# Attention and mixture-of-experts block: another order of value products, side products and the copy of av_bank within a step of the attention loop

## What is computed

```python
xn = layernorm(x)                                   # x: 8 x 512 tokens x 128, f32
h = xn @ W1 + b1                                    # 16 heads, q, k, v of 8 columns each
w = softmax(causal(q @ k.T / sqrt(8)))
att = (w @ v) @ Wp + bp
shared = (silu(xn @ sg.T) * (xn @ su.T)) @ sd.T     # 352 hidden columns
routed = sum over the 2 best of 8 experts of weight * ffn_expert(xn)
out = x + att + shared + routed
```

## Time and profile before

| | us |
|---|---|
| median of 3 runs | 559.99 |
| the runs | 559.99, 562.06, 555.53 |
| profiled execution, its own time | 559.99 |
| its span, first to last instruction | 558.3 |
| TensorE busy | 513.5 |
| mean granted TensorE clock | 0.955 |

### The profile page before, as it was taken

How to read it: one execution, slowest core, us unless ns; L and a number is a source line. 1 busy time by engine, 2 the same in 40 slices (tenths; PEclk the granted TensorE clock), 3 DMA queues, 4 the chain that set the end, 5 groups by cost and what they waited for, 6 DMA issues and landing times.

```text
span 558.3 us, 13933 instructions
## 1 busy us (share of the span) xinstructions
PE 513.5 (92%) x4584; PEld 332.5 (60%) x4585; DVE 398.1 (71%) x753; ACT 310.4 (56%) x684; POOL 324.7 (58%) x382
## 2 busy tenths in 40 slices
PE   8888999889998998899989889999999999999995
PEld 3334444444444444343443348999999999977673
DVE  7886668887878777877887675565555555548896
ACT  2016777777767767777776753333333333365542
POOL 5439742342466777767777744667666444575442
PEclk9875999999979989999997989999999999999998
DMA  5416631040211245522211112211221222434554
GB/s 166 157 46 197 211 143 65 21 154 3 77 60 44 94 170 196 176 71 90 78 54 36 49 34 65 68 57 57 73 59 57 62 70 57 119 108 130 155 153 147
DMA packets 52156, 53.46 MB, mean 96 GB/s; under 512 B 5744, under 2 KB 39568, under 8 KB 51856
## 3 DMA queue, kind: packets, MB, share of 16 engines
q1 hardware_dynamic: 47616, 43.71, 24.7%
q0 software_dynamic: 4352, 8.95, 4.8%
q10 hardware_dynamic: 144, 0.20, 0.1%
HBM read 20.38 MB, written 17.90 MB: 69 GB/s over the span
## 4 chain that ended last, share of the span: by engine, by line
PE 66%; DVE 12%; ACT 7%; issue 6%; DMA 4%; POOL 3%; DVEq 1%; SPq 0%; ACTq 0%; POOLq 0%
PE av_bank L879 13%; PE mx_pair L824 9%; PE av_bank L1053 9%; PE st_banks L852 5%; DVE neg_max L1543 4%; PE st_banks L1064 4%; DVE o_sb L1719 3%; ACT probs L1244 3%; PE av_bank L902 2%; PE st_banks L759 2%; PE mx_pair L1039 2%; DMA out<-o_sb 2%; PE mx_pair L1043 2%; PE mx_pair L1044 2%; PE mx_pair L1042 2%
## 5 line engine op out<-in xcount | busy, mean ns | idle before, releaser
L1543 DVE TENSOR_REDUCE neg_max<-mx_pair 128x2 f32<-128x256 f32 (+3 forms) x256 | 203.7, 822 | 63.4 <-PE mx_pair L835 61.0
L1244 ACT ACTIVATE probs<-st_banks 128x512 f32<-128x512 f32 (+1 forms) x384 | 181.0, 524 | 63.7 <-PE st_banks L852 62.0
L705 POOL DMA_INDIRECT y_tok<-y_sb,y_rows x72 | 70.0, 972 | 74.1 <-ACT y_sb L1349 59.6
L852 PE MATMUL st_banks<-q_st,k_st 32*128 32x128 f32 (+3 forms) x512 | 96.3, 407 | 13.4 <-ACT probs L1244 7.7
L824 PEld LDWEIGHTS mx_pair<-k_st,q_st 31*128 31x128 f32 x512 | 43.4, 190 | 101.8 <-issue 62.7
L879 PE MATMUL av_bank<-probs,v_wide 128*18 128x384 f32 (+3 forms) x1024 | 98.9, 461 | 3.5 <-ACT av_sb L1257 2.6
L824 PE MATMUL mx_pair<-k_st,q_st 31*128 31x256 f32 (+3 forms) x512 | 90.1, 395 | 11.3 <-DVE neg_max L1543 11.1
L629 POOL DMA_INDIRECT sorted_x<-xn_rows,slot_idx x64 | 63.8, 997 | 13.3 <-issue 12.7
L1342 ACT ACTIVATE sg<-mx_pair 128x352 f32<-128x352 f32 x72 | 33.4, 463 | 62.3 <-PE mx_pair L1044 62.3
L852 PEld LDWEIGHTS st_banks<-q_st,k_st 32*128 32x128 f32 x512 | 48.2, 191 | 27.5 <-ACT probs L1244 18.6
L588 POOL TENSOR_SCALAR_AFFINE_SELECT probs<-probs 128x1024 f32<-128x1024 f32 x32 | 35.0, 1094 | 45.8 <-ACT probs L1244 45.7
(11 more groups left out here) (214 smaller groups left out, 895.9 us busy)
## 6 DMA issues: line engine op xcount, KB each, us to landing
sorted_x<-zeros SPq DMA_DIRECT2D x8, 580.5 KB, 4.1
xg<-sorted_x SPq DMA_DIRECT2D x36, 129.0 KB, 2.2
picked<-y_tok SPq DMA_DIRECT2D x16, 256.0 KB, 3.7
q_st<-q_hi SPq DMA_DIRECT2D x14, 256.0 KB, 2.5
k_st<-k_hi SPq DMA_DIRECT2D x14, 256.0 KB, 2.5
egu_lo<-in_e_gu SPq DMA_DIRECT2D x2, 1408.0 KB, 6.6
x_all<-in_x SPq DMA_DIRECT2D x8, 256.0 KB, 3.6
att_T<-a_T SPq DMA_DIRECT2D x8, 256.0 KB, 2.1
```

Source lines behind the costliest of these rows:

```text
L705: pool.indirect_dma_start(y_tok, bass.IndirectOffsetOnAxis(ap=y_rows[:, t, k:k + 1], axis=0), y_sb[t % 2][:, k, :], None).then_inc(y_st[t ...
L852: ins = pe.matmul(st_banks[:, i % 3, lo:lo + w], k_st[buf][32 * j:32 * j + 32, g, kb * P:(kb + 1) * P], q_st[buf][32 * j:32 * j + 32, g, k ...
L1244: act.activation(dst, src, ACT.Exp, scale=SCALE).then_inc(st_free, 1)
L1543: ins = dve.tensor_reduce(neg_max[:, g, h:h + 2, qb], mx_pair[i % 2][:, :, lo:lo + (qb + 1) * P], AX.X, ALU.max, negate=True)
```

## The change

Three things move, in TensorE's program, in ScalarE's program and in the table that numbers the fills of st_banks:
- values(.,1) takes the place of values(.,3), and values(.,3) and (.,2) follow together behind mm2, ahead of M3.
- The first extras come ahead of M4 and the second extras ahead of M5; M5 with S(8,9) is the last of the step.
- On ScalarE the copy of av_bank goes behind exponents (6,7), and the copies of the extras follow the new order.

```diff
-        order += scored[0:4] + ([("m", s + 1)] if -1 <= s < GROUPS - 1 else []) + scored[4:10] + first_misc(s) + scored[10:12] + second_misc(s)
+        order += scored[0:4] + ([("m", s + 1)] if -1 <= s < GROUPS - 1 else []) + scored[4:8] + first_misc(s) + scored[8:10] + second_misc(s) + scored[10:12]
...
-                if kb in (1, 3):
+                if kb == 1:
                     pe.wait_ge(masked, 3 * n + 2)
...
                 if valued:
-                    values(s - 1, 3)
+                    values(s - 1, 1)
                 if maxima:
                     max_scores(s + 2, 2)
...
                 if valued:
-                    values(s - 1, 1)
+                    values(s - 1, 3)
+                    values(s - 1, 2)
                 if maxima:
                     max_scores(s + 2, 3)
                 if scored:
                     scores(s, (4, 5))
                 if maxima:
                     max_masks(s + 2, 3)
-                if valued:
-                    values(s - 1, 2)
-                if maxima:
-                    max_scores(s + 2, 4)
-                if scored:
-                    scores(s, (10, 11))
-                if maxima:
-                    max_masks(s + 2, 4)
...
                 if maxima:
-                    max_scores(s + 2, 5)
+                    max_scores(s + 2, 4)
                 if scored:
-                    scores(s, (8, 9))
+                    scores(s, (10, 11))
                 if maxima:
-                    max_masks(s + 2, 5)
+                    max_masks(s + 2, 4)
...
                 if s == 12:
                     value_bias()
+                if maxima:
+                    max_scores(s + 2, 5)
+                if scored:
+                    scores(s, (8, 9))
+                if maxima:
+                    max_masks(s + 2, 5)
...
                 if scored:
                     exponents(s, (6, 7))
+                if s >= 1 and s % GP == 0:
+                    results_out_of(s - 1)
                 if scored:
                     exponents(s, (4, 5))
-                if scored:
-                    exponents(s, (10, 11))
...
                 if s % 4 == 1 and s <= 25:
                     values_out((s + 3) // 4)
+                if scored:
+                    exponents(s, (10, 11))
...
-                if scored:
-                    exponents(s, (8, 9))
-                if s >= 1 and s % GP == 0:
-                    results_out_of(s - 1)
...
                 if s == 12:
                     bias_out()
+                if scored:
+                    exponents(s, (8, 9))
```

## The result

The change made the kernel slower: 563.44 us against 559.94 (medians of 15 runs each), ratio 1.0065 with a 95% interval of 1.0038 to 1.0093. Forecast were 558.3 us and "within 1%". The time lies just inside the range (552.8 to 563.5); the direction was wrong. The profiled execution took 564.77 us, 4.78 more than that of before, with a span of 563.0 and a mean granted clock of 0.931 against 0.955.

A forecast was written before the change was run, and what follows sets the result against it. The loop was taken as a chain of hand-overs that make TensorE wait, no engine full. Steps 1 to 25 give -1.8, later plain pairs +0.2, the start 0: in all -1.7, 559.99 to 558.3 us; range 552.8 to 563.5.

The forecast's parts named there:

- the walk: Four attention steps timed from trace durations: 34.21 us against 34.50, -1.7 in all, plain-step idle time unchanged; chance 0.47.
- Rival B: New stops in plain even steps let the clock fall in steps 8, 20, 24, 26, 30: +12, 570 us; chance 0.07.
- The price of a dip: Clock dips in the attention loop: the first costs 2.4 us, the other two about 1.2 and 2.4.
- Part 1: Moving the av_bank copy behind exponents (6,7) removes 0.33 us before values(.,0) in 15 odd steps, 5 us at most.
- Part 2: values(.,2) ahead of scores (4,5) uncovers a wait of scores (10,11): 0.5 us in plain odd steps, 0.7 in plain even.
- Parts 3 and 4: First extras (about 1.1 us) cover the wait before scores (10,11), returning part of 0.58; second extras delay M5 and exponent 8.
- The start: Steps -2 to 4, with up to two x transposes each, not walked: 0, bounded by -1 and +1 us.
- "Nothing gained" (A): Copy ahead of exponents (4,5) and uncovered scores (10,11) take back all: 560 us, 562 at worst; chance 0.25.
- the dips gone (C): The loop's three clock dips vanish as stops go and projections fill the middle: -6.0, 552.3 us; chance 0.15.
- the third mask (D): The earlier values(.,2) waits for its mask from GpSimd, 18 steps x 0.3 = +5.4: 563.7 us; chance 0.06.

The follow-up runs named there:

- after_fill5: The changed kernel plus four needless products a step in steps without first extras, ahead of scores (10,11), (8,9) and the next M0: 548.6 us, 0.9769 of before.
- hybrid: The changed kernel, but in steps without first extras values(.,2) stands last and the av_bank copy behind exponents (4,5): 577.02 us, 1.0125 of before.
- after_again: The changed kernel as it is, run again beside before on chip Q: 573.91 us, 1.008 of before.
- after_third: The changed kernel as it is, run once more beside before on chip P: 575.24 us, 1.0111 of before.
- misc_only: The kernel before with only the extras moved, values products and av_bank copy as before: 579.62 us, 1.0197 of before.
- before_stop: The kernel before, but scores (10,11) wait for one exponent more in steps from 5 on without first extras: 576.38 us, 1.0129 of before.

## Why the prediction was wrong

**The step that failed** is the sentence "My walk leaves the total idle time of a plain step as it was, so there is no term for the clock in the sum". The total was about right; that only the total mattered was not. Between the marks of step 4 and step 30, after_fill5 gives the new order at nearly full clock: 219.94 us, less some 1.5 for its one dip (steps 11 and 12), 218.4. For before, the steps with dips put at their full-clock length give 223.4. So the dips cost 231.3 - 218.4 = 12.9 us in after and 228.9 - 223.4 = 5.5 in before, +7.4, against a gain of 223.4 - 218.4 = 5.0: together the +2.4. This split is an estimate: it takes the steps of after_fill5, from another chip and with products, for those that after would have had without dips, and rests on the rows above, where the products delay nothing. Per microsecond at the lower level that is 12.9 / 34.1 = 0.38 and 5.5 / 17.1 = 0.32, so the 10.2 us more behind the loop's step 29 make 3.3 to 3.9 and explain its +3.35.

The second step that failed is the size of the gain: the walk had 1.6 for steps 4 to 29, and it was 5.0. The two errors stand against each other, which is why 563.44 still lies 0.06 us inside the range. That is luck.

**Rival B happened**, given a chance of 0.07: the clock falls in steps 8, 20, 24 and 26, where it had held, and it "decides from three more dips on"; there were six more in the loop. Of B's list step 30 was wrong, since before already had a dip at its end (320.5 us). What spoke against B in the prediction, equal total idle, was no argument. Its 570 was too high because the gain was larger than the walk's: -0.97 - 5.0 + 7.4 + 3.35 = 4.8 is what the profiled execution has.

**The price of a dip** held: 2.4 in the prediction, 19.42 - 17.02 = 2.4 for steps 20 and 21 against before, 2.8 against the 16.66 that the two take in after_fill5. Three dips at 6.0 were 5.5. The Trainium skill (TensorE: Matmul & The Clock Gate, "A second HAM failure mode: psum-queue depth-cycling") tells of another kernel in which short idle spells between groups of products were frequent enough to make the clock go back and forth. The trace agrees: in the 10 us ahead of the dip in step 20 no stop is longer than 0.66 us. The prediction drew on another section of that page, and only for the step's total.

**Part 1** (the copy): the wait is gone as forecast. **Part 2**: 0.7 forecast for the plain even step, 0.66 measured. **Parts 3 and 4**: right in kind, undersized; for v with features the walk had 0.05 more than before, and it became 0.18 less. For q the walk had waits of 0.2, 0.6 and 0.3 at (10,11), (8,9) and M0; step 22 of after:

```profile
246.97 1.12 PE L759 MATMUL st_banks<-xnT,wqkv 128*128 128x512 f32 x2
...
248.44 0.39 PE L852 MATMUL st_banks<-q_st,k_st 32*128 32x256 f32 x2
...
249.36 0.38 PE L852 MATMUL st_banks<-q_st,k_st 32*128 32x256 f32 x2 [0.35 <-ACT probs L1243]
...
250.01 0.49 PE L824 MATMUL mx_pair<-k_st,q_st 31*128 31x512 f32 x2 [0.26 <-DVE neg_max L1542]
250.28 0.50 PE L852 MATMUL st_banks<-q_st,k_st 32*128 32x512 f32 x2
```

They are 0, 0.35 and 0.26, half a microsecond less, and the step takes 8.28 for the 8.57 of the walk; where the other 0.2 went is open. k came out at 8.41 for 8.59, v with features at 8.89 for 9.12; I did not follow those two line by line. Four steps at full clock take 7.79 + 8.88 + 8.28 + 8.40 = 33.35 us (after_fill5, whose plain step holds products) where the walk had 34.21 and before has 34.52: a gain of 1.2 in these four (20 to 23) instead of 0.3. The groups before step 16 gain 0.7 to 1.0. The start (0, bounded by 1) gave 0.97 in this profile. "Nothing gained" (A), the dips gone (C) and the third mask (D) did not happen.

**What to carry.** Where a trace shows an engine's clock going up and down, its idle time must be counted by stretch and not by step: moving stops together can cost more than removing some of them gives. What exactly starts a dip these runs don't show (hybrid). Price every re-ordering twice, at full clock from undisturbed steps and by the number of dips. And where stops can't be removed, needless products that fit into them are a cheap test of whether the clock is what is paid for, and with the new order here also the better kernel, on two chips of three.

## What the runs showed that I had not expected

- **Chips differ by 10 us.** The same kernel before takes 560 to 561 us on R and S and 570 to 571 on P and Q, at a clock lower by 0.014. That accounts for 4.6 us of it, at 3.3 per 0.01.
- **On P and Q the new order has a delay of its own.** In the new orders q steps from 14 on, the steps in which GpSimd sends scatters, take 9.3 us at full clock, for 8.3 in the first profile. The traces show where it arises. The row of the 16 products of values(.,3) and (.,2) and the row of the copy of av_bank behind them, in q step 22, first in after_again (chip Q), then in after:

```profile
250.70 0.85 PE L879 MATMUL av_bank<-probs,v_wide 128*18 128x128 f32 x16
...
252.84 0.60 ACT L1256 ACTIVATE av_sb<-av_bank 128x512 f32<-128x512 f32 x1 [0.79 <-PE av_bank L879]
```

```profile
245.66 0.85 PE L879 MATMUL av_bank<-probs,v_wide 128*18 128x128 f32 x16
...
246.71 0.61 ACT L1256 ACTIVATE av_sb<-av_bank 128x512 f32<-128x512 f32 x1
```

Of what the copy waits for, the last of these products comes last. The copy starts 0.20 us after their recorded end in after and 1.29 in after_again. (The recorded ends are modelled; the signal that releases the copy is not.) In after_again and after_third the copy starts 0.9 to 2.0 us after that end in all even steps from 14 to 28, and about 0.2 or less in the even steps before; in after and after_fill5 it is about 0.2 throughout. hybrid, on P, has values(.,2) in its new place only in steps with extras: in its q steps 14, 18 and 22 the signal comes 1.2 us after the end, in its plain steps 16, 20 and 24 at once (in 28 it is late by 0.9). In misc_only and before_stop, which have the old place on the same two chips, it comes at most 0.33 us after, but for one step (1.1). So what is late is the pair values(.,3), values(.,2) in its new place, from step 14 on, on two of the chips. Why, no run shows. It is the likely reason why the change gains nothing at equal clock there, and why after with products is at 0.977 and 0.985 on two chips and at 1.003 on the third. A ratio of one chip is not that of another.
- At equal clock the change is even with before on P and Q. On chips like R and S the line through before gives 567.6 us at the 0.934 of its first runs, which took 563.3 on average: a gain of 4.3 there. The line is extended for it, since no run of before on R and S has a clock below 0.946.
- The new order with products that compute nothing is up to 2.3% shorter than before. Whether others, placed or counted differently, do better was not tried.
